# One more pair by seven products, and engine programs written run by run, in a two-group matrix kernel

## The chip, the cores and the metric

One NeuronCore of a Trainium2 chip runs the kernel. The metric is the device time of one execution in microseconds, the median of several runs.

## The reference

The input r_x holds 1024 rows of 10240 numbers; each row is two vectors of 5120. Both go through the same two layers, are joined and go through a third, and a dot product ends it:

```python
x = x.reshape(-1, 2 * F)                      # F = 5120
x1, x2 = (x[:, :F], x[:, F:])
h1 = leaky_relu(layer_norm(x1 @ W1.T))        # W1: 256 x 5120, leaky_relu(x) = max(0.05 x, x)
h2 = leaky_relu(layer_norm(x2 @ W1.T))
h1 = leaky_relu(layer_norm(h1 @ W2.T))        # W2: 64 x 256
h2 = leaky_relu(layer_norm(h2 @ W2.T))
h = jnp.concatenate([h1, h2], axis=-1)
h = leaky_relu(layer_norm(h @ W3.T))          # W3: 8 x 128
return h @ W4.T                               # W4: 1 x 8
```

Layer norm subtracts the mean over the outputs and divides by the root of the mean square. Nearly all of the arithmetic is the first layer, 2048 vectors of 5120 times W1.

## The kernel before

**Tiling.** F is cut into 20 pairs of two blocks of 128. The 2048 vectors are two groups (g) of 1024, each of two blocks (b) of NC = 512 columns; the 256 outputs are two halves (m) of 128. For a group and a pair, TensorE multiplies a 2 x 2 matrix of weight blocks with a 2 x 2 matrix of x blocks and sums over the 20 pairs in PSUM, whose eight banks hold 128 x 512 each.

**Precision.** Each operand is split into a rounded high part and a low part, and each product is three matmuls: high by high, high by low, low by high. ScalarE makes the high part by a cast (`hi`, L443), VectorE the low part by a subtraction (`lo`, L524). Weights are centred first: ScalarE takes the mean (L399) and subtracts it (L405), VectorE makes the low part (L539).

**Two kinds of pair.** An E unit multiplies plainly: eight products, 24 matmuls, in two halves (c) of 12. An S unit uses seven products of sums (Strassen-Winograd), 21 matmuls: first R, three raw blocks, nine matmuls; then T, four sums of blocks, twelve matmuls. VectorE makes the sums of x (L575, L580, L585) and of the weights (L551, L556, L561); their high parts are `hi` (1478 ns for R, 1903 for T) and L427 for the weight, their low parts `lo` and L530. The products of S pairs go to banks P1, P5, P6, P7 and others and are put together at a group's end by four additions (`seven_into`, L593 to L601), to which the eight-product banks are added (`eight_into`, L607).

**Order.** `ORDER` lists the units; TensorE takes them as they stand: group 0 is E E, four times S E E, S E, S E E L; group 1 is F, E, eight times S E, D. L is the last E of group 0 (its two halves are cast into T's buffer), F the first of group 1, after which layer 2 of group 0 runs, and D is two pairs at the end. Group 0 prepares weights; group 1 finds them in SBUF, save those of the `MIXED` pairs that are S only there. All engines follow one count of parts: `hi_ready`, `lo_ready` and `used` are one semaphore each, so ScalarE, VectorE and TensorE must take the parts in the same order. In one pass of ScalarE's loop stand: cast of unit u's first part, weight of the next unit, cast of u's second part, weight high part of the next. In VectorE's pass before an S: low part of the first half, the sums of the S with the second half's low part before the last of them, then the S's weight low part.

**Buffers.** The parts have one pair of high and low buffers each: R, T, E0, E1. `hi` waits (`used`) until TensorE is done with the old content. Raw x lies in rings of two (S, 1 MB) and four (halves of E, 512 KB), raw weights in a ring of three (256 KB). SP's queue issues all loads but the first half of x, which ScalarE's issues; each waits for the low part of the ring's earlier owner.

**What the prediction's steps touch:** `ORDER` and `plan`; the programs of ScalarE (`start_w`, `end_w`, `hi`, `copy_p1`) and VectorE (`lo`, `w_lo`, the sums, `seven_into`, `centre_w23`), and SP's loads. `centre_w23` centres the small weights, after unit 8.

Of the kernel before, what the change touches and what calls it, by code (L numbers as in the profile page):

```python
# [12 lines left out]
P = 128  # L13
# [12 lines left out]
SEVEN = 6  # L26
MIXED = 2
# [7 lines left out]
W23_UNIT = 8  # L35
# [7 lines left out]
ORDER = ("EE" + "SEE" * 4 + "SE" + "SEEL", "FE" + "SE" * 8 + "D")  # L43
# [26 lines left out]
class Part:  # L70

    n: int
# [9 lines left out]
def plan():  # L82
    units, latest, count, halves, sevens = [], {}, 0, 0, 0
    for g, order in enumerate(ORDER):
        seen = {"S": 0, "E": 0}
        for kind in order:
# [16 lines left out]
            parts = []  # L103
            for buffer, p, c, blocks in wanted:
                parts.append(Part(count, g, buffer, p, c, blocks, latest.get(buffer, 0), halves))
                count += 1
                if kind != "S" and blocks[-1] == 1:
                    halves += 1
            for part in parts:
                latest[part.buffer] = part.n + 1  # L110
# [16 lines left out]
def following(u):  # L127
    return UNITS[u.n + 1] if u.n + 1 < len(UNITS) else None
# [11 lines left out]
def rec_kernel(nc, x, w1, w2, w3, w4, out):  # L140
    with ExitStack() as ctx:
# [88 lines left out]
        hi_ready = sem("hi_ready")  # L230
        lo_ready = sem("lo_ready")
        used = sem("used")
# [32 lines left out]
        def w_slot(u):  # L265
            return W_AT[u.n] % W_RING, 16 * (W_AT[u.n] // W_RING + 1)

# [31 lines left out]
        def _(sp):  # L299
# [13 lines left out]
            def load_seven(nth):  # L313
                if nth >= len(SEVENS):
                    return
                u = SEVENS[nth]
                s, landed = s_slot(u)
                if nth >= S_RING:
                    sp.wait_ge(lo_ready, SEVENS[nth - S_RING].parts[0].n + 1)
                sp.dma_start(xs_raw[:, s, :], x[u.g, u.pair]).then_inc(xs_landed[s], 16)  # L320

            def load_half(half):
                if half not in HALVES:
                    return
                part = HALVES[half]
                s, landed = e_slot(half)
                block0 = 2 * part.c
                if half >= E_RING:
                    sp.wait_ge(lo_ready, HALVES[half - E_RING].n + 1)
                sp.dma_start(xe_raw[:, s, :], x[part.g, part.pair, :, block0 * NC:(block0 + 2) * NC])\  # L330
                    .then_inc(xe_landed[s], 16)
# [6 lines left out]
            load_half(2)  # L338
            load_half(3)
            load_w(2)  # L340
            load_seven(0)
            for u in UNITS:
                if u.kind == "S":
                    load_seven(u.nth + S_RING)
                else:
                    load_half(u.parts[-2].half + E_RING)
                if u.n == 0:
                    load_w(W_RING)
                    load_seven(1)
                if u.n + 1 + W_RING < len(FIRST):  # L350
                    load_w(u.n + 1 + W_RING)
                if u.kind != "S":
                    load_half(u.parts[-1].half + E_RING)
                if u.n == 4:
# [4 lines left out]
                if u.n == len(FIRST) + 6:  # L359
# [36 lines left out]
        def _(act):  # L396
# [11 lines left out]
            def start_w(u):  # L408
                s, landed = w_slot(u)
# [14 lines left out]
            def end_w(u):  # L424
                if u.kind == "S":
# [3 lines left out]
            def hi(u, part):  # L429
                if u.kind != "S":  # L430
                    s, landed = e_slot(part.half)
                    if part.n == 0:
# [8 lines left out]
                if part.before:  # L441
                    act.wait_ge(used, part.before)
                act.copy(hi_of(u, part), raw_of(u, part)).then_inc(hi_ready, 1)  # L443

            def copy_p1(g):
                act.wait_ge(used, last_seven(g).parts[0].n + 1)
# [4 lines left out]
            def leak1(g, b, m):  # L451
                act.wait_ge(drained, 5 * g + 2 + 2 * b + m)
                act.activation(a1[:, b, m, :], h1[:, b, m, :], ACT.Prelu, alpha=LEAK).then_inc(a1_ready, 1)  # L453

# [11 lines left out]
            act.dma_start(xe_raw[:, 0, 0:NC], x[0, u.pair, :, 0:NC]).then_inc(first_x_landed, 16)  # L466
            act.dma_start(xe_raw[:, 0, NC:], x[0, u.pair, :, NC:2 * NC]).then_inc(xe_landed[0], 16)
# [10 lines left out]
            for u in UNITS[1:]:  # L478
                nxt = following(u)
                prepare_w = nxt and nxt.n in W_AT  # L480
                hi(u, u.parts[0])
                if u.n == len(FIRST) - 2:
                    copy_p1(0)
                if prepare_w:
                    start_w(nxt)
                hi(u, u.parts[1])
                if prepare_w:
                    end_w(nxt)
                if u.kind == "F":
                    for b in range(B):  # L490
                        for m in range(M):
                            leak1(u.g - 1, b, m)
                        for m in range(M):
                            square1(u.g - 1, b, m)
                if u.n == len(FIRST) + 1:
                    for b in range(B):
                        layer2_end(0, b)
                if u.kind == "D":
                    copy_p1(u.g)
                    hi(u, u.parts[2])  # L500
                    hi(u, u.parts[3])
# [12 lines left out]
        def _(dve):  # L514
# [7 lines left out]
            def lo(u, part):  # L522
                dve.wait_ge(hi_ready, part.n + 1)
                dve.tensor_tensor(lo_of(u, part), raw_of(u, part), hi_of(u, part).bitcast(F32), ALU.subtract)\  # L524
                    .then_inc(lo_ready, 1)

            def w_lo(u):
                if u.kind == "S":
# [37 lines left out]
            def two_sums(u):  # L566
                s, landed = s_slot(u)
                dve.wait_ge(xs_landed[s], landed)
                if u.nth:
                    dve.wait_ge(lo_ready, SEVENS[u.nth - 1].parts[1].n + 1)  # L570
# [16 lines left out]

            def seven_into(g, k):

                if k == 0:  # L590
                    dve.wait_ge(used, last_seven(g).parts[1].n + 1)
# [5 lines left out]
                if k == 2:  # L597
                    dve.tensor_tensor(h1[:, 0, 1, :], h1[:, 1, 1, :], acc[:, P7, :], ALU.add).then_inc(h1_step, 1)
# [70 lines left out]
            for u in UNITS[1:]:  # L669
                nxt = following(u)  # L670
                prepare_w = nxt and nxt.n in W_AT
                g = u.g
                if u.kind == "S":
                    lo(u, u.parts[0])
                    if prepare_w:
                        w_lo(nxt)
                    lo(u, u.parts[1])
                elif u.kind == "D":
                    for part in u.parts:
                        lo(u, part)  # L680
                    for k in range(4):
                        seven_into(g, k)
                elif u.n == len(FIRST) - 2:
                    lo(u, u.parts[0])
                    w_lo(nxt)
                    seven_into(g, 0)
                    seven_into(g, 1)
                    lo(u, u.parts[1])
                    seven_into(g, 2)
                    seven_into(g, 3)  # L690
                elif u.n == len(FIRST) + 1:
                    lo(u, u.parts[0])
                    lo(u, u.parts[1])
                    two_sums(nxt)
                    third_sum(nxt)
                    fourth_sum(nxt)
                elif nxt.kind == "S":
                    lo(u, u.parts[0])
                    if prepare_w:
                        w_two_sums(nxt)  # L700
                    two_sums(nxt)
# [280 lines left out]
```

## Time and profile before

| what | value |
|---|---|
| median of 3 runs | 254.1 us (253.92 to 254.76) |
| the profiled execution | 255.57 us |
| its span, first to last instruction | 253.8 us |
| PE busy | 233.0 us, 1022 matmuls |
| DVE (VectorE) busy | 195.6 us |
| ACT (ScalarE) busy | 153.5 us |
| mean granted clock of TensorE | 0.984 |

PE's busy time counts matmuls to their modelled ends, which overlap, so 233.0 is not a measure of how full it is; the distance from start to start is. A number in brackets in a timeline is the idle time before the instruction and who ended it.

### The profile page before, as it was taken

How to read it: one execution, taken by the hardware profiler on the slowest of the kernel's cores; microseconds unless marked ns; L12 is line 12 of the kernel's file. 1: busy time of each engine (PE TensorE's matmuls, PEld its weight loads, DVE VectorE, ACT ScalarE, POOL GpSimd, SP SyncE). 2: the span in 40 equal slices, each digit the busy share in tenths (PEclk: the TensorE clock that was granted, in tenths of full speed). 3: DMA queues.
4: the chain of work that ended last, by engine and by line, in shares of the span. 5: the costliest groups of instructions: out<-in, count | busy, mean ns of one | idle time of the engine just before them, and what ended most of it. 6: DMA issues, size and time to landing. Idle time of an engine off the chain costs nothing.

```text
span 253.8 us, 2896 instructions
## 1 busy us (share of the span) xinstructions
PE 233.0 (92%) x1022; PEld 183.5 (72%) x1022; DVE 195.6 (77%) x250; ACT 153.5 (60%) x239; POOL 8.3 (3%) x16
## 2 busy tenths in 40 slices
PE   5987997997997988989999999999999999999982
PEld 1765875875865866868677888888888888888662
DVE  1689599598699499985965878999887999619434
ACT  4869379379478577858476536464546677333620
POOL 1000000000000000000000031000000000000023
PEclk9999999999999999999999999999999999999985
DMA  5999747656666567665482543787666425220000
GB/s 182 414 407 393 256 145 275 217 176 240 205 206 216 209 203 233 192 224 171 159 262 87 181 149 111 256 316 269 209 211 223 154 79 165 80 85 4 0 0 1
DMA packets 13550, 47.99 MB, mean 189 GB/s; under 512 B 1888, under 2 KB 2272, under 8 KB 11744
## 3 DMA queue, kind: packets, MB, share of 16 engines
q1 hardware_dynamic: 13248, 47.29, 54.4%
q10 hardware_dynamic: 288, 0.52, 0.7%
q8 instruction: 8, 0.13, 0.2%
q14 instruction: 6, 0.05, 0.1%
HBM read 47.80 MB, written 0.00 MB: 188 GB/s over the span
## 4 chain that ended last, share of the span: by engine, by line
PE 52%; DVE 18%; ACT 18%; issue 5%; DMA 4%; SPq 1%; POOL 1%; POOLq 0%; ACTq 0%; DVEq 0%
PE acc L766 48%; DVE xt_lo L524 7%; ACT xt_hi L443 4%; DMA xs_raw<-x 4%; ACT xr_hi L443 3%; ACT unused L399 3%; DVE x_sum L575 3%; ACT xe_hi L443 2%; PE acc L897 2%; DVE xe_lo L524 2%; ACT we_hi L405 1%; DVE x_sum L580 1%; ACT stage L405 1%; PE acc L885 1%; ACT x_sum L453 1%
## 5 line engine op out<-in xcount | busy, mean ns | idle before, releaser
L443 ACT CAST xe_hi<-xe_raw 128x1024 fp32r<-128x1024 f32 (+1 forms) x49 | 50.5, 1031 | 47.8 <-PE acc L766 44.0
L524 DVE TENSOR_TENSOR xe_lo<-xe_raw,xe_hi 128x1024 fp32r<-128x1024 f32 (+1 forms) x49 | 58.8, 1199 | 26.0 <-ACT xe_hi L443 25.9
L766 PE MATMUL acc<-xe_lo,we_hi 128*128 128x512 f32 x176 | 69.0, 392 | 1.1 <-DVE xe_lo L524 1.1
L766 PE MATMUL acc<-xe_hi,we_lo 128*128 128x512 f32 x176 | 68.6, 390 | 0.0
L766 PE MATMUL acc<-xe_hi,we_hi 128*128 128x512 f32 x176 | 48.3, 391 | 0.3 <-PE acc L766 0.3
L766 PEld LDWEIGHTS acc<-xe_lo,we_hi 128*128 128x128 f32 x176 | 33.0, 188 | 9.8 <-issue 3.1
L766 PEld LDWEIGHTS acc<-xe_hi,we_hi 128*128 128x128 f32 x176 | 32.9, 188 | 7.4 <-issue 0.7
L766 PEld LDWEIGHTS acc<-xe_hi,we_lo 128*128 128x128 f32 x176 | 33.0, 188 | 6.8
L524 DVE TENSOR_TENSOR xt_lo<-x_sum,xt_hi 128x2048 fp32r<-128x2048 f32 x14 | 32.1, 2290 | 7.3 <-ACT xt_hi L443 7.3
L443 ACT CAST xt_hi<-x_sum 128x2048 fp32r<-128x2048 f32 x14 | 26.6, 1903 | 8.9 <-DVE x_sum L585 5.2
L766 PE MATMUL acc<-xt_lo,ws_hi 128*128 128x512 f32 x56 | 22.3, 398 | 6.7 <-DVE xt_lo L524 6.7
L443 ACT CAST xr_hi<-xs_raw 128x1536 fp32r<-128x1536 f32 x14 | 20.7, 1478 | 6.8 <-PE acc L766 6.8
L524 DVE TENSOR_TENSOR xr_lo<-xs_raw,xr_hi 128x1536 fp32r<-128x1536 f32 x14 | 24.5, 1752 | 0.0
L766 PE MATMUL acc<-xt_hi,ws_lo 128*128 128x512 f32 x56 | 21.9, 390 | 0.0
L766 PE MATMUL acc<-xr_lo,ws_hi 128*128 128x512 f32 x42 | 16.9, 402 | 2.5 <-DVE xr_lo L524 2.5
L766 PEld LDWEIGHTS acc<-xt_lo,ws_hi 128*128 128x128 f32 x56 | 10.5, 188 | 11.1 <-issue 9.1
L399 ACT ACTIVATE unused<-stage 128x256 f32<-128x256 f32 x40 | 16.3, 408 | 1.7 <-DMA stage<-w 1.6
L575 DVE TENSOR_TENSOR x_sum<-xs_raw 128x1024 f32<-128x1024 f32 x14 | 17.1, 1219 | 0.3 <-DMA xs_raw<-x 0.3
L766 PE MATMUL acc<-xr_hi,ws_lo 128*128 128x512 f32 x42 | 16.4, 392 | 0.0
L427 ACT CAST ws_hi<-stage 128x896 fp32r<-128x896 f32 x8 | 7.6, 945 | 13.4 <-DVE stage L561 13.4
L766 PE MATMUL acc<-xt_hi,ws_hi 128*128 128x512 f32 x56 | 15.1, 391 | 0.0
L379 POOL TENSOR_TENSOR inv<-var,minus_half 128x4 f32<-128x4 f32 (+1 forms) x3 | 4.9, 1625 | 239.4 <-DVE var L622 239.4
(87 smaller groups left out, 269.3 us busy)
## 6 DMA issues: line engine op xcount, KB each, us to landing
xe_raw<-x SPq DMA_DIRECT2D x51, 512.0 KB, 3.9
xs_raw<-x SPq DMA_DIRECT2D x14, 1024.0 KB, 5.1
stage<-w SPq DMA_DIRECT2D x21, 256.0 KB, 4.7
xe_raw<-x ACTq DMA_DIRECT2D x2, 256.0 KB, 5.0
stage<-w SPq DMA_DIRECT2D x2, 128.0 KB, 4.2
w_raw<-w SPq DMA_DIRECT2D x1, 64.0 KB, 3.3
w_sb<-w SPq DMA_DIRECT2D x1, 8.0 KB, 3.1
w_sb<-w SPq DMA_DIRECT2D x1, 16.0 KB, 3.0
```

The source lines that it names most:

```text
L379: pool.tensor_tensor(inv12[:, a * J:b * J], var12[:, a * J:b * J], minus_half[:, a * J:b * J], ALU.pow)\
L399: act.activation(unused[:, c, :], w_raw[:, s, c * N1:(c + 1) * N1], ACT.Copy, scale=-1.0 / N1, accum_out=w_mean[:, u.pair, c:c + 1]).then_ ...
L405: return act.activation(to, w_raw[:, s, c * N1:(c + 1) * N1], ACT.Identity, bias=w_mean[:, u.pair, c:c + 1], scale=1.0)
L427: act.copy(ws_hi[:, u.pair, :], w_mid[:, P:]).then_inc(w_hi_ready, 1)
L443: act.copy(hi_of(u, part), raw_of(u, part)).then_inc(hi_ready, 1)
L453: act.activation(a1[:, b, m, :], h1[:, b, m, :], ACT.Prelu, alpha=LEAK).then_inc(a1_ready, 1)
L524: dve.tensor_tensor(lo_of(u, part), raw_of(u, part), hi_of(u, part).bitcast(F32), ALU.subtract)\
L575: dve.tensor_tensor(x_sum[:, 0:2 * NC].rearrange("p (a n) -> p a n", a=2), raw[:, :, 0, :], b12, ALU.add).then_inc(two_sums_ready, 1)
L580: dve.tensor_tensor(x_sum[:, 2 * NC:3 * NC], x_sum[:, 0:NC], x_block(u, 2), ALU.add)\
L766: return pe.matmul(acc[:, bank, :], w, x, start=first, stop=True, skip_group_check=True)
L885: ins = pe.matmul(h2_ps[b][h * N2:(h + 1) * N2, :], w2_sb[:, m, :], a1[:, b, m, h * T * P:(h + 1) * T * P], start=(m == 0), stop=(m == M - ...
L897: ins = pe.matmul(acc[:, var1_bank[g][b], k:k + 1], sq1_sum[b][:, j * P:(j + 1) * P], ones[:], start=True, stop=True)
```

## The change

Group 0 has seven instead of six S pairs, and group 1 one instead of two mixed ones (`SEVEN`, `MIXED`); group 1 has eight as before. Group 0's order becomes E E, twice S E E, four times S E, S E E L. The one count of parts becomes one per buffer (`hi_ready[buffer]` and so on), so an engine's program may leave TensorE's order. The programs are written by runs: a run is the E units up to an S, that S, and the units after it. ScalarE casts R of the S, then, in turn, the halves of the run's second E, the S's weight and T, and then the weights and halves of the next run's first E and the weight of the next S. VectorE makes all sums of the S first, then the low parts in that order. At the groups' crossing `seven_into` stands ahead of the low parts, at the end too, and ScalarE's leaks stand ahead of its squares. Layer 3 of group 0 stands between two halves of an E. The first half of x is loaded by SP's queue, and the halves of an E lie one after another in DRAM. `centre_w23` moves to the run of the fifth S.

```diff
-SEVEN = 6
-MIXED = 2
+SEVEN = 7
+MIXED = 1
-ORDER = ("EE" + "SEE" * 4 + "SE" + "SEEL", "FE" + "SE" * 8 + "D")
+ORDER = ("EE" + "SEE" * 2 + "SE" * 4 + "SEEL", "FE" + "SE" * 8 + "D")
...
+def runs():
+
+    starts = [0] + [u.n + 1 for u in SEVENS]
+    ends = [u.n for u in SEVENS] + [len(UNITS)]
+    es = [UNITS[a:b] for a, b in zip(starts, ends)]
+    return list(zip(es, SEVENS + [None], es[1:] + [[]]))
...
+def crosses(run):
+
+    return run[0].g != run[-1].g
...
-        hi_ready = sem("hi_ready")
-        lo_ready = sem("lo_ready")
-        used = sem("used")
+        hi_ready = {buffer: sem("hi_ready_" + buffer) for buffer in x_hi}
+        lo_ready = {buffer: sem("lo_ready_" + buffer) for buffer in x_hi}
+        used = {buffer: sem("used_" + buffer) for buffer in x_hi}
...
+            first_half = x_half_of(0, pair, 0)
             sp.dma_start(w_raw[:, 0, 0:N1], w1[pair, :, 0:N1]).then_inc(first_w_landed, 16)
+            sp.dma_start(xe_raw[:, 0, 0:NC], first_half[:, 0:NC]).then_inc(first_x_landed, 16)
             sp.dma_start(w_raw[:, 0, N1:], w1[pair, :, N1:]).then_inc(w_landed[0], 16)
+            sp.dma_start(xe_raw[:, 0, NC:], first_half[:, NC:]).then_inc(xe_landed[0], 16)
...
+            for i, (es, n, after) in enumerate(RUNS):
+                if not n:
+                    copy_p1(GROUPS - 1)
+                    for part in es[1].parts:
+                        hi(es[1], part)
+                    break
+                if crosses(es):
+                    copy_p1(es[0].g)
+                    start_w(es[2])
+                    for k in range(2):
+                        for u in es[1:3]:
+                            hi(u, u.parts[k])
+                    for part in es[3].parts:
+                        hi(es[3], part)
+                    layer1_end(es[0].g)
+                    for part in es[4].parts:
+                        hi(es[4], part)
...
+                    hi(n, n.parts[0])
+                    hi(n, n.parts[1])
+                else:
+                    if i:
+                        hi(n, n.parts[0])
+                    for j, u in enumerate(es[1:], 1):
+                        if j > 1:
+                            start_w(u)
+                        hi(u, u.parts[0])
+                        if i == 0:
+                            start_w(n)
+                        elif j == 1:
+                            end_w(n)
+                            hi(n, n.parts[1])
+                        hi(u, u.parts[1])
+                    if i == 0:
+                        hi(n, n.parts[0])
+                    if i == 0 or len(es) == 1:
+                        end_w(n)
+                        hi(n, n.parts[1])
+                start_w(after[0])
+                hi(after[0], after[0].parts[0])
+                if len(after) > 1:
+                    start_w(after[1])
+                hi(after[0], after[0].parts[1])
+                start_w(RUNS[i + 1][1])
...
+            for i, (es, n, after) in enumerate(RUNS):
+                g = es[0].g
+                if not n:
                     for k in range(4):
                         seven_into(g, k)
...
+                    for part in es[1].parts:
+                        lo(es[1], part)
+                    break
+                if crosses(es):
                     seven_into(g, 0)
                     seven_into(g, 1)
...
+                    w_lo(es[2])
                     seven_into(g, 2)
                     seven_into(g, 3)
...
+                    for k in range(2):
+                        for u in es[1:3]:
+                            lo(u, u.parts[k])
+                    for part in es[3].parts:
+                        lo(es[3], part)
...
+                elif i == 0:
+                    lo(es[1], es[1].parts[0])
+                    lo(es[1], es[1].parts[1])
+                    sums(n)
+                    lo(n, n.parts[0])
+                else:
+                    sums(n)
+                    for j, u in enumerate(es[1:], 1):
+                        if j > 1:
+                            w_lo(u)
+                        lo(u, u.parts[0])
+                        if j == 1:
+                            lo(n, n.parts[0])
+                        lo(u, u.parts[1])
+                    if len(es) == 1:
+                        lo(n, n.parts[0])
+                w_lo(n)
+                lo(n, n.parts[1])
...
+                w_lo(after[0])
+                lo(after[0], after[0].parts[0])
+                if crosses(es):
                     layer3(1, 0, B, small[:, B * J:B * J + B * J * N3])
+                lo(after[0], after[0].parts[1])
...
+                if len(after) > 1:
+                    w_lo(after[1])
+                if es[0].n == W23_UNIT + 2:
+                    centre_w23()
...
+    for g, sevens in enumerate((SEVEN, BOTH)):
+
+        x[g, sevens:] = x[g, sevens:].reshape(-1, P, 2, 2 * NC).transpose(0, 2, 1, 3).reshape(-1, P, 4, NC)
+    x = x.reshape(GROUPS, PAIRS, P * 4 * NC)
```

`sums` is the six additions of an S, weights and x in turn; `layer1_end` is the four leaks and then the four squares.

## Rows read from the trace of the kernel before

**Rows 1.** The chain that ended last, merged: start, length, what
```profile
147.21 79.05 PE acc L766 x348
```

**Rows 2.** Table of stages: stretch, its length, busy time (instructions) by engine, clock, DMA, GB/s
```profile
38.52:56.90 18.38, 16.48 (x70) 12.69 (x69) 14.34 (x18) 12.92 (x26) 0.00 (x0) 1.00 0.66 219
...
93.66:106.03 12.37, 10.77 (x47) 8.26 (x45) 11.79 (x14) 9.90 (x20) 0.00 (x0) 1.00 0.70 220
```

**Rows 3.** Waits of the whole span: engine and tile, awaited; total us, times, longest
```profile
ACT xe_hi L443 <- PE acc L766: 44.0, 22, 6.4
DVE xe_lo L524 <- ACT xe_hi L443: 25.9, 12, 6.3
```

**Rows 4.** Timeline of PE: start, length, line, operation [idle before]
```profile
108.17 1.09 PE L766 MATMUL acc<-xt_hi,ws_hi 128*128 128x512 f32 x4
110.38 0.47 PE L766 MATMUL acc<-xt_lo,ws_hi 128*128 128x512 f32 x1 [1.13 <-DVE xt_lo L524]
```

**Rows 5.** Timeline of VectorE in the SE cycle, same columns
```profile
99.58 0.42 DVE L551 TENSOR_TENSOR stage<-stage 128x256 f32<-128x256 f32 x1
...
103.79 1.08 DVE L530 TENSOR_TENSOR ws_lo<-stage,ws_hi 128x896 fp32r<-128x896 f32 x1
104.79 1.75 DVE L524 TENSOR_TENSOR xr_lo<-xs_raw,xr_hi 128x1536 fp32r<-128x1536 f32 x1
106.46 0.88 DVE L539 SCALAR_TENSOR_TENSOR we_lo<-stage,w_mean,we_hi 128x256 fp32r<-128x256 f32 x2
107.94 2.29 DVE L524 TENSOR_TENSOR xt_lo<-x_sum,xt_hi 128x2048 fp32r<-128x2048 f32 x1 [0.60 <-ACT xt_hi L443]
110.15 1.22 DVE L524 TENSOR_TENSOR xe_lo<-xe_raw,xe_hi 128x1024 fp32r<-128x1024 f32 x1
111.29 0.87 DVE L539 SCALAR_TENSOR_TENSOR we_lo<-stage,w_mean,we_hi 128x256 fp32r<-128x256 f32 x2
112.08 1.22 DVE L524 TENSOR_TENSOR xe_lo<-xe_raw,xe_hi 128x1024 fp32r<-128x1024 f32 x1
```

**Rows 6.** Timeline of ScalarE in the SE cycle
```profile
102.17 0.95 ACT L427 CAST ws_hi<-stage 128x896 fp32r<-128x896 f32 x1 [2.47 <-DVE stage L561]
103.02 1.48 ACT L443 CAST xr_hi<-xs_raw 128x1536 fp32r<-128x1536 f32 x1
104.40 0.42 ACT L399 ACTIVATE unused<-stage 128x256 f32<-128x256 f32 x1
...
106.01 1.90 ACT L443 CAST xt_hi<-x_sum 128x2048 fp32r<-128x2048 f32 x1
107.81 1.06 ACT L443 CAST xe_hi<-xe_raw 128x1024 fp32r<-128x1024 f32 x1
108.75 0.43 ACT L399 ACTIVATE unused<-stage 128x256 f32<-128x256 f32 x1
```

**Rows 7.** The page's list of DMA issues: count, KB each, median us to landing
```profile
stage<-w SPq DMA_DIRECT2D x21, 256.0 KB, 4.7
```

**Rows 8.** Timelines of ScalarE and VectorE at the start
```profile
13.85 1.04 ACT L443 CAST xe_hi<-xe_raw 128x1024 fp32r<-128x1024 f32 x1
...
16.87 1.22 DVE L524 TENSOR_TENSOR xe_lo<-xe_raw,xe_hi 128x1024 fp32r<-128x1024 f32 x1
```

**Rows 9.** Timeline of VectorE: first step of the small weights' centring, first after it
```profile
61.70 0.28 DVE L649 TENSOR_REDUCE w_mean<-w_raw 128x2 f32<-128x128 f32 x1
...
62.97 1.22 DVE L524 TENSOR_TENSOR xe_lo<-xe_raw,xe_hi 128x1024 fp32r<-128x1024 f32 x1
```

**Rows 10.** Timeline of PE: first products of unit F
```profile
130.46 0.70 PE L766 MATMUL acc<-xe_hi,we_hi 128*128 128x512 f32 x2 [0.30 <-PE acc L766]
```

**Rows 11.** Timeline of GpSimd after the crossing
```profile
148.15 2.48 POOL L379 TENSOR_TENSOR inv<-var,minus_half 128x8 f32<-128x8 f32 x1 [146.49 <-DVE var L622]
```

**Rows 12.** Timelines of VectorE and PE at the end
```profile
234.83 1.29 DVE L607 TENSOR_TENSOR stage<-acc,stage 128x512 f32<-128x512 f32 x2
...
233.79 0.39 PE L766 MATMUL acc<-xe_lo,we_hi 128*128 128x512 f32 x1
```

More of the change, by code:

```diff
@@ L82, in plan @@
 def plan():
-    units, latest, count, halves, sevens = [], {}, 0, 0, 0
+    units, made, halves, sevens = [], {}, 0, 0
     for g, order in enumerate(ORDER):
@@ L103, in plan @@
             parts = []
+            before = dict(made)
             for buffer, p, c, blocks in wanted:
-                parts.append(Part(count, g, buffer, p, c, blocks, latest.get(buffer, 0), halves))
-                count += 1
+                made[buffer] = made.get(buffer, 0) + 1
+                parts.append(Part(made[buffer], g, buffer, p, c, blocks, before.get(buffer, 0), halves))
                 if kind != "S" and blocks[-1] == 1:
                     halves += 1
-            for part in parts:
-                latest[part.buffer] = part.n + 1
             units.append(Unit(len(units), g, kind, pair, sevens, parts))
@@ L124 @@
 W_SEVENS = {u.n: i for i, u in enumerate(v for v in W_WORK if v.kind == "S")}
[L127 to L128 removed]
+def runs():
[3 more added lines that the diff above has]
+    return list(zip(es, SEVENS + [None], es[1:] + [[]]))
+RUNS = runs()
+def crosses(run):
+    return run[0].g != run[-1].g
 def last_seven(g):
@@ L338, in _ @@
             load_half(2)
+            load_w(2)
             load_half(3)
-            load_w(2)
             load_seven(0)
[L342 to L354, printed above, removed]
+            load_w_after(UNITS[0])
+            load_halves(UNITS[0], 1)
+            load_halves(UNITS[0], 2)
+            load_seven(1)
+            load_w_after(UNITS[1])
+            for es, n, after in RUNS:
+                if n:
+                    load_w_after(n)
+                for j, u in enumerate(es[1:], 1):
+                    if j > 1:
+                        load_w_after(u)
+                    for k in range(len(u.parts)):
+                        load_halves(u, k)
+                        if n and j == 1 and k == 0 and not crosses(es):
+                            load_seven(n.nth + S_RING)
+                if n and (len(es) == 1 or crosses(es)):
+                    load_seven(n.nth + S_RING)
+                for j, u in enumerate(after[:2]):
+                    load_w_after(u)
+                    if j == 0:
+                        for k in range(len(u.parts)):
+                            load_halves(u, k)
+                if es[0].n == W23_UNIT:
                     sp.dma_start(w2_raw[:], w2).then_inc(small_landed, 16)
@@ L431, in hi @@
                     s, landed = e_slot(part.half)
-                    if part.n == 0:
+                    if part is UNITS[0].parts[0]:
                         act.wait_ge(first_x_landed, 16)
@@ L441, in hi @@
                 if part.before:
-                    act.wait_ge(used, part.before)
-                act.copy(hi_of(u, part), raw_of(u, part)).then_inc(hi_ready, 1)
+                    act.wait_ge(used[part.buffer], part.before)
+                act.copy(hi_of(u, part), raw_of(u, part)).then_inc(hi_ready[part.buffer], 1)
             def copy_p1(g):
-                act.wait_ge(used, last_seven(g).parts[0].n + 1)
+                act.wait_ge(used["R"], last_seven(g).parts[0].nth)
                 if g == 0:
@@ L586, in fourth_sum, with sums @@
                     .then_inc(sums_ready, 1)
+            def sums(u):
+                new_w = u.n in W_AT
+                if new_w:
+                    w_two_sums(u)
+                two_sums(u)
+                if new_w:
+                    w_third_sum(u)
+                third_sum(u)
+                if new_w:
+                    w_fourth_sum(u)
+                fourth_sum(u)
             def seven_into(g, k):
                 if k == 0:
-                    dve.wait_ge(used, last_seven(g).parts[1].n + 1)
+                    dve.wait_ge(used["T"], last_seven(g).parts[1].nth)
                     dve.wait_ge(p1_copied, g + 1)
@@ L803, in seven @@
                         ins = multiply(u.g, bank, w_of(ws_lo, n), x_of(x_hi, k))
-                    ins.then_inc(used, 1)
+                    ins.then_inc(used[part.buffer], 1)
             def w_of(buffers, part, m):
@@ L832, in eight @@
                             ins = e_lo(u, part, b, m)
-                    ins.then_inc(used, 1)
+                    ins.then_inc(used[part.buffer], 1)
             def first_eight(u):
@@ L844, in first_eight @@
                             ins = e_lo(u, part, b, m)
-                    ins.then_inc(used, 1)
+                    ins.then_inc(used[part.buffer], 1)
             def last_eight(u):
```

135 lines of the change are left out of this document (45 added, 90 removed).

## The prediction

> **What bounds the kernel now.** I read the table of stages first. In the second half of the program TensorE runs without a gap: 348 matmuls of 128x512 in 79.05 us, 0.227 us each [rows 1]. So a half pair of eight-product work (12 matmuls) is 2.72 us, an eight-product pair (E) 5.45, a seven-product pair (S) with 21 matmuls 4.77, and a cycle SEE should take 69 x 0.227 = 15.7 us. A cycle of the first group takes 18.38 us for that [rows 2], and there are four such cycles, one SE cycle of 12.37 us (10.2 by count) and an end. The waits say why: ScalarE stands 44.0 us waiting for TensorE before it casts a half (xe_hi), and VectorE 25.9 us for that cast [rows 3]. A buffer of the high part is free only once TensorE has used it; ScalarE's program has the half next, so the seven-product pair's weight and its cast stand behind it, and VectorE, which has the sums after the half, idles too and then does everything late. TensorE shows the end of it: the four high products of a pair's sums start at 108.17, but the low ones only at 110.38 instead of 109.08 [rows 4]. With such gaps at R, T and the second half, the cycle loses 2.7 us. None of the three engines is full: the lost time is order.
>
> **What VectorE and ScalarE need at least.** Starts are closer than durations (a 1.22 us subtraction is followed after 1.14), so I take start to start. VectorE [rows 5]: all sums of an S with its weight 103.79 - 99.58 = 4.21, less one half's subtraction of 1.14 that lies among them, 3.07; weight low part 1.00; R low 1.67; T low 2.21: together 7.95 for an S. An E is 0.79 for the weight and 2 x 1.14 for the halves, 3.07. ScalarE [rows 6]: weight high part 0.85, R 1.38, mean and centre 1.61, T 1.80, a half 0.94; 5.64 for an S, 3.49 for an E. Per SEE: TensorE 15.7, VectorE 14.1, ScalarE 12.6. Per SE: 10.2, 11.0, 9.1. So with a good order SEE is TensorE's, SE is VectorE's.
>
> **The change, part by part.** (1) One E of group 0 becomes an S: TensorE 3 matmuls less, -0.7 us; VectorE 7.95 - 3.07 = 4.9 more; ScalarE 2.1 more. In group 1 the reverse happens only to weights: one seven-product weight less, where VectorE has time. (2) The order of units becomes two SEE cycles and four SE cycles. (3) In the new programs the sums of an S stand before the half of the E ahead of it, and the casts of the first E after an S stand before that run ends. VectorE has then 3.07 us of work in the place where it idles now. (4) A count per buffer costs no instruction; it lets the orders differ from TensorE's. (5) The halves lie together in DRAM: 4 KB per partition as before. I take nothing; a load of a weight lands in 4.7 us [rows 7], and in the walk below every load is asked for over 8 us ahead, which hides a change either way. (6) The first x loads go from ScalarE's queue to SP's, two issues ahead of the others (about 0.4 us each). The first cast stands behind the weight's centring and waits for that; the S's first 1 MB comes after 3.75 MB of loads in either order. I take 0; the bounds are -0.3 and +0.9 us, the two issues, for both engines stand at the start.
>
> **The walk through group 0.** Today the low part of the last half before the first S stands behind that S's first sums: cast at 13.85 to 14.89, subtraction only at 16.87 [rows 8]. After the change it goes at 14.93, and VectorE starts the sums at 16.07. From there to the end of the last S's T low part VectorE has seven S, 7 x 7.95 = 55.7; eight E between them, 24.6; and the centring of the small weights, moved into this stretch, 1.27 [rows 9]: 16.07 + 81.5 = 97.6 if it never waits. I walked the three programs step by step with the steps above, 0.04 us from ScalarE to VectorE (T cast ends 107.91, subtraction starts 107.94 [rows 5, 6]), 0.15 from VectorE to TensorE (110.23 to 110.38 [rows 4, 5]), and, an estimate, a buffer free 0.25 after the start of TensorE's next product. VectorE waits 0.6 and 0.4 us in the first SEE cycle (casts behind ScalarE's weights), and 0.8 and 0.8 in the second (buffers not yet free), 2.6 in all. So T low ends at 100.2, where it ends for the sixth S today at 110.2. The seven S end on TensorE at 26.1, 42.9, 58.5, 68.8, 79.0, 91.4 and 102.4: cycles of 16.7 and 15.7, two of 10.2 in which VectorE's lead of 1.9 us is used up (0.8 each), one of 12.4 (0.8, the centring and the rest of the lead), one of 11.0. ScalarE's own loop in SE, from a ready weight over the sums (2.6), weight high, T, two weights and two halves is 10.5 us, under VectorE's 11.0, so it does not set the cycle.
> Then E, E, L. VectorE now puts the four additions of group 0's seven-product banks and L's weight ahead of the second E's low parts; with ScalarE's copy of bank P1 waiting on the last weight, the first low part comes at 109.7 where TensorE wants it at 108.8: 1.0 us lost. Behind that copy on ScalarE are L's weight and four casts; TensorE waits for these, and the 1.0 contains it. L starts at 114.4 and F at 119.8; F starts at 130.46 now [rows 10]. That is -10.6 us.
>
> **Crossing and group 1.** The additions to the eight-product banks, squares and layer 2 keep their order against TensorE. After S7 the layer 3 steps now stand between the two halves of an E, behind GpSimd's 2.48 us power [rows 11]: the second half's low part ends about 1.3 us before it is wanted, the next S's T low part about 0.3 after: +0.3 (bounds 0 and 2.5, if all of the power falls on the path). The rest of group 1 is VectorE 9 to 10.2 us against 10.2: no gap, as now.
>
> **The end.** The four additions move ahead of the last low parts. Today the first addition to an eight-product bank starts at 234.83 behind them, though the product that it needs starts at 233.79 and ends near 234.2 [rows 12]. It can go at 234.25: -0.5 us, next limited by that product.
>
> The sum: -10.6 + 0.3 - 0.5 = -10.8. The profiled execution took 255.57 us with a span of 253.8; the median is 254.1. So the span becomes 243.0, the profiled execution about 244.8, the median 243.3.
>
> **A rule weighed against a row.** In rows 5 an instruction starts 0.08 us before its predecessor's duration is over, also where sums wait for sums with other work between. The Trainium skill, "VectorE: DVE Perf Modes", section "The DRAIN you can't avoid", says that the next operation does not start until the pipeline has emptied, and adds that one that is not held starts earlier. The steps of this trace bear out the second half. If the first held for the new order, rival A would come.
>
> **Rivals.** (A) VectorE pays full durations, or waits as much again between steps, since almost each of its steps now has another engine's result in front of it. By durations an S is 8.7 us and an E 3.3: 7 x 0.75 + 8 x 0.25 = 7.2 us more, of which the 2.6 of waiting take about 1.7: +5.5, 248.8 us. For it: VectorE is the bound and nothing hides it. Against: in the SE stretch of the trace the steps stay close.
> (B) The change does not do what it says, and ends slower: the gap at each S stays. ScalarE still waits for TensorE's buffers, and its weight and T cast stand behind that wait, so the low T part stays last. Then there are seven gaps of 2.7 instead of six: +2.7 - 0.7 = +2.0, 256.1 us. It decides from 2.4 us per S ((6 x 2.7 + 0.7) / 7); at exactly that the time is unchanged. For it: 44.0 us of such waits today. Against: VectorE has the sums to do meanwhile, and the walk finds T ready ahead in three of the seven.
> (C) Loads late. A weight is asked for when the slot three units back is done: in the walk at 28.5 for 37.2, 8.7 us ahead. Landing takes 4.7 us [rows 7]. Each landing over 8.7 us stretches some six rounds of the ring; at 10.5 us the whole gain is gone, at 11 it is 257 us. Against: the rate rises only from 219 GB/s [rows 2] to about 240 (3.75 MB in 15.7 us).
>
> **How the numbers follow.** The walk holds: 0.71, own range 240.7 (VectorE never waits) to 246.4 (start +0.9, crossing +2.2). A: 0.14. B: 0.08, half of it with gaps that leave the time as it is. C: 0.03. Over half the gain lost by something else, 249 to 253: 0.04. The range, 240.7 to 249.0, takes in the walk and A. This kernel can tell about 0.3% (0.8 us) from no change. Faster by over 0.3%: 0.71 + 0.14 + 0.04 = 0.89; within 0.3%: 0.04, of B; slower: 0.04 of B and 0.03 of C, 0.07.
>
> **What would show it.** PE's stretch from one S to the next: 15.7 us in SEE, 11 in SE; VectorE over 95% busy from 55 to 100 us; no idle of VectorE of 3 us before a half. F's first product near 120 us. Group 1 without gaps, but for 0.3 us after S7. If VectorE's steps in SE sum to 12 us, A. If its idle before halves is still over 2 us per cycle, B. If ScalarE waits for w or x, C.

## The result, and the profile after

The changed kernel takes 244.96 us (244.87 to 245.41, 4 runs) against 254.43 (253.92 to 255.15, 4 runs): a ratio of 0.9629, 95% interval 0.9600 to 0.9658, 9.5 us less. Forecast were 243.3 us and a range of 240.7 to 249.0. The profiled execution took 244.94 us, with a span of 243.1 where 243.0 had been walked out.

The table of stages of the profile after, columns as in [rows 2] (stretch, its length, busy time with instructions for PE, PE's weight load, VectorE, ScalarE, GpSimd, clock, DMA, GB/s):

```profile
37.90:53.63 15.73, 15.73 (x70) 12.87 (x69) 14.24 (x18) 11.92 (x22) 0.00 (x0) 1.00 0.76 251
53.63:63.84 10.21, 10.21 (x46) 8.45 (x45) 10.21 (x14) 7.54 (x15) 0.00 (x0) 1.00 0.69 234
...
55.00:100.00 45.00, 43.04 (x187) 34.44 (x186) 44.93 (x60) 35.96 (x68) 0.00 (x0) 1.00 0.70 233
```

The first line is a whole SEE cycle: 15.73 us where [rows 2] has 18.38. The last holds the four SE cycles: VectorE is busy 44.93 of 45.00 us. It has become the bound there, and TensorE is what idles (43.04 busy). The waits of the whole span (engine and tile, awaited; total, times, longest) answer [rows 3]:

```profile
ACT xe_hi L479 <- PE acc L845: 22.6, 14, 4.9
ACT xt_hi L479 <- DVE x_sum L650: 17.4, 7, 5.1
DVE xe_lo L587 <- ACT xe_hi L479: 15.4, 19, 1.7
PEld acc L845 <- DVE ws_lo L595: 4.6, 4, 1.8
PE acc L845 <- DVE ws_lo L595: 3.2, 3, 1.3
```

ScalarE's wait for TensorE is halved, VectorE's wait for that cast falls from 25.9 to 15.4 us and has no longer stretch than 1.7. New are the last two lines: TensorE waits for the low part of an S's weight. They show a wait that my walk did not have (below).

VectorE's timeline of one SE cycle (start, length, line, operation [idle before]), from the first weight sum to the next one, as in [rows 5]:

```profile
57.74 0.42 DVE L616 TENSOR_TENSOR stage<-stage 128x256 f32<-128x256 f32 x1
...
60.82 1.75 DVE L587 TENSOR_TENSOR xr_lo<-xs_raw,xr_hi 128x1536 fp32r<-128x1536 f32 x1
62.49 1.08 DVE L595 TENSOR_TENSOR ws_lo<-stage,ws_hi 128x896 fp32r<-128x896 f32 x1
63.49 2.28 DVE L587 TENSOR_TENSOR xt_lo<-x_sum,xt_hi 128x2048 fp32r<-128x2048 f32 x1
65.70 0.87 DVE L604 SCALAR_TENSOR_TENSOR we_lo<-stage,w_mean,we_hi 128x256 fp32r<-128x256 f32 x2
66.49 2.35 DVE L587 TENSOR_TENSOR xe_lo<-xe_raw,xe_hi 128x1024 fp32r<-128x1024 f32 x2
68.76 0.41 DVE L616 TENSOR_TENSOR stage<-stage 128x256 f32<-128x256 f32 x1
```

The cycle is 68.76 - 57.74 = 11.02 us without a gap, and the sums take 3.08. Only TensorE's waits are left to show; its timeline at the first, the sixth and the seventh S and at the crossing:

```profile
21.14 0.64 PE L845 MATMUL acc<-xr_lo,ws_hi 128*128 128x512 f32 x1 [1.33 <-DVE ws_lo L595]
...
86.92 0.50 PE L845 MATMUL acc<-xr_lo,ws_hi 128*128 128x512 f32 x1 [1.33 <-DVE ws_lo L595]
...
97.94 0.50 PE L845 MATMUL acc<-xr_lo,ws_hi 128*128 128x512 f32 x1 [0.50 <-DVE ws_lo L595]
...
110.24 0.47 PE L845 MATMUL acc<-xe_lo,we_hi 128*128 128x512 f32 x1 [1.17 <-DVE xe_lo L587]
...
120.79 0.70 PE L845 MATMUL acc<-xe_hi,we_hi 128*128 128x512 f32 x2 [0.30 <-PE acc L845]
```

The last line is F's first product, at 130.46 in [rows 10]. From the first product of group 1's first S (the prediction's S7: it counts the S from zero there) the chain that ended last holds one piece without a gap; for [rows 1]:

```profile
137.53 90.06 PE acc L845 x396
```

396 products in 90.06 us are 0.227 each, as before.

### The profile page after: what moved, and what is told of

It reads as the page before. It is cut to its first block, busy times and chain, and to the rows that moved or that the text cites. A ratio compares the mean times of both kernels' runs of the same rounds, so it can differ in the third digit from the quotient of the medians.

```text
span 243.1 us, 2884 instructions
## 1 busy us (share of the span) xinstructions
PE 229.5 (94%) x1019; PEld 182.6 (75%) x1019; DVE 198.8 (82%) x251; ACT 153.0 (63%) x237; POOL 8.3 (3%) x16
## 4 chain that ended last, share of the span: by engine, by line
PE 61%; DVE 25%; ACT 7%; issue 3%; DMA 2%; POOL 1%; SPq 1%; POOLq 0%; DVEq 0%; ACTq 0%
PE acc L845 57%; DVE xe_lo L587 5%; DVE xt_lo L587 4%; DVE xr_lo L587 3%; ACT xe_hi L479 2%; DVE x_sum L640 2%; DMA xe_raw<-x 2%; DVE ws_lo L595 2%; DVE we_lo L604 2%; PE acc L976 2%; ACT unused L433 1%; DVE x_sum L645 1%; PE acc L964 1%; ACT xt_hi L479 1%; DVE x_sum L650 1%
## 5 line engine op out<-in xcount | busy, mean ns | idle before, releaser
L587 DVE TENSOR_TENSOR xe_lo<-xe_raw,xe_hi 128x1024 fp32r<-128x1024 f32 (+1 forms) x47 | 55.6, 1198 | 15.4 <-ACT xe_hi L479 15.4
L479 ACT CAST xe_hi<-xe_raw 128x1024 fp32r<-128x1024 f32 (+1 forms) x47 | 47.8, 1026 | 28.8 <-PE acc L845 22.6
L479 ACT CAST xt_hi<-x_sum 128x2048 fp32r<-128x2048 f32 x15 | 28.6, 1910 | 17.4 <-DVE x_sum L650 17.4
L587 DVE TENSOR_TENSOR xt_lo<-x_sum,xt_hi 128x2048 fp32r<-128x2048 f32 x15 | 34.3, 2287 | 2.2 <-ACT xt_hi L479 2.2
L587 DVE TENSOR_TENSOR xr_lo<-xs_raw,xr_hi 128x1536 fp32r<-128x1536 f32 x15 | 26.2, 1750 | 0.0
L845 PE MATMUL acc<-xr_lo,ws_hi 128*128 128x512 f32 x45 | 18.5, 411 | 3.2 <-DVE ws_lo L595 3.2
L845 PE MATMUL acc<-xr_hi,ws_lo 128*128 128x512 f32 x45 | 18.3, 406 | 0.0
L845 PE MATMUL acc<-xt_hi,ws_hi 128*128 128x512 f32 x60 | 16.6, 399 | 0.0
L845 PE MATMUL acc<-xr_hi,ws_hi 128*128 128x512 f32 x45 | 13.0, 397 | 1.1 <-ACT ws_hi L463 0.9
L845 PEld LDWEIGHTS acc<-xt_hi,ws_hi 128*128 128x128 f32 x60 | 11.8, 196 | 2.6
```

The source lines that it names most:

```text
L479: act.copy(hi_of(u, part), raw_of(u, part)).then_inc(hi_ready[part.buffer], 1)
L845: return pe.matmul(acc[:, bank, :], w, x, start=first, stop=True, skip_group_check=True)
```

## The experiments

In all of them ratios are against the kernel before on the same chip. Single executions of one kernel spread over 1 to 2.7 us here, so times decide only where the intervals stand apart, and else I compare stretches inside profiles. Much of the spread is in two places that no experiment here aims at: the start, and the clock in the last 8 us (last section).

**1. The new programs with six S.** The kernel takes all of the change but the seventh pair.

```diff
-SEVEN = 7
-MIXED = 1
+SEVEN = 6
+MIXED = 2
-ORDER = ("EE" + "SEE" * 2 + "SE" * 4 + "SEEL", ...
+ORDER = ("EE" + "SEE" * 4 + "SE" + "SEEL", ...
-                if es[0].n == W23_UNIT + 2:
+                if es[0].n == W23_UNIT + 3:
```

> The new programs with six S pairs and the old order of units. Theory (VectorE bounds group 0, so the seventh S costs 2.2 us: TensorE would need 4 x 15.7 + 10.2 = 73.0 us from the end of the first S to the end of the last, where the changed kernel took 102.2 - 26.9 = 75.2): 242.8 us, that is faster than the changed kernel. Rival (the seventh S saves its three matmuls): 245.7 us.

Measured: 242.34 us, 0.9511 (0.9474 to 0.9548), clearly under the changed kernel's 0.9629 (0.9600 to 0.9658): 2.6 us by the medians, 3.0 by the ratios. By the profiles the seventh S itself costs less. From the first S's T low part to the last S's it is 75.22 us with six and 76.79 with seven, and from there to layer 2 of group 0 both take the same, so 1.6 us are the seventh S's. The rest of the 2.9 us between the two spans is a start 0.7 earlier and 0.6 in the last 8 us, where the clock fell sooner in the changed kernel's profile. Table of stages from 55 to 97 us, where here SEE cycles run, and one SE cycle from 83 to 95:

```profile
55.00:97.00 42.00, 41.79 (x184) 34.00 (x183) 38.98 (x53) 31.29 (x59) 0.00 (x0) 1.00 0.73 236
```

VectorE is busy 38.98 of 42 and TensorE has hardly a gap.

**2. The old programs with seven S** in the new order of units.

```diff
-SEVEN = 6
-MIXED = 2
+SEVEN = 7
+MIXED = 1
-ORDER = ("EE" + "SEE" * 4 + "SE" + "SEEL", ...
+ORDER = ("EE" + "SEE" * 2 + "SE" * 4 + "SEEL", ...
```

> The old programs with seven S pairs and the new order of units. Theory (the gain is the programs'; under the old ones a cycle SEE takes 18.4 us and an SE 11.7): last S ends 2 x 18.4 + 4 x 11.7 = 83.6 us after the first instead of 4 x 18.4 + 11.7 = 85.3: 252.7 us. Rival (the gap stays at every S, 2.7 us each): 256 us. If the order of units and the seventh S brought most of the gain: under 249.

Measured: 253.97 us, 0.9969 (0.9949 to 0.9990), 0.8 us faster. VectorE's T low parts:

```profile
59.41 2.29 DVE L524 TENSOR_TENSOR xt_lo<-x_sum,xt_hi 128x2048 fp32r<-128x2048 f32 x1 [0.58 <-ACT xt_hi L443]
...
72.36 2.29 DVE L524 TENSOR_TENSOR xt_lo<-x_sum,xt_hi 128x2048 fp32r<-128x2048 f32 x1 [0.59 <-ACT xt_hi L443]
...
84.06 2.29 DVE L524 TENSOR_TENSOR xt_lo<-x_sum,xt_hi 128x2048 fp32r<-128x2048 f32 x1 [0.60 <-ACT xt_hi L443]
```

The second SE cycle is the 11.7 us expected, the first 12.95: the centring of the small weights stands in it, and I had not counted that. It is the 1.3 us by which the kernel is slower than the 252.7 expected. So the gain of the change is the programs', and under them the seventh pair takes some of it back, while under the old ones it gave a little.

**3. Spare work for VectorE** in the SE runs of group 0, and in a second kernel in those of group 1 (`== 1` in place of `== 0`).

```diff
+                if es[0].g == 0 and len(es) == 1:
+                    dve.tensor_tensor(spare[:], ws_hi[:, 0, 0:NC].bitcast(F32), ws_hi[:, 0, 0:NC].bitcast(F32), ALU.add)
```

> The changed kernel with one addition of 128x512 on VectorE, of no use, at the end of each run with one E in group 0 (four of them, 0.61 us each from start to start). Theory (VectorE bounds that stretch): +2.4 us less what little lead is left, 246.9 to 247.4. Rival (ScalarE's loop or the weight loads bound it): 245.0 to 245.5.

> The same addition in the runs with one E of group 1 instead. TensorE bounds that stretch and VectorE has 9.1 to 10.2 us of work in 10.2: no change, 245.0, or up to 0.6 more where the last S also brings a weight.

Measured: 246.29 us, 0.9669 (0.9628 to 0.9710), and 244.83, 0.9611 (0.9570 to 0.9652). The first interval overlaps the changed kernel's, so I read the profile. T's low parts of the third and of the seventh S end 45.31 us apart in the changed kernel and 47.12 apart here; with the addition in group 1, 45.32. Only three of the four additions lie between the two (I had counted four): 1.81 us, 0.60 each, all of it on the path.

```profile
65.95 2.35 DVE L588 TENSOR_TENSOR xe_lo<-xe_raw,xe_hi 128x1024 fp32r<-128x1024 f32 x2
68.22 0.68 DVE L814 TENSOR_TENSOR spare<-ws_hi 128x512 f32<-128x512 f32 x1
68.82 0.41 DVE L617 TENSOR_TENSOR stage<-stage 128x256 f32<-128x256 f32 x1
```

**4. The centring moved** from the SE stretch to the crossing.

```diff
-                    for part in es[3].parts:
-                        lo(es[3], part)
+                    lo(es[3], es[3].parts[0])
+                    centre_w23()
+                    lo(es[3], es[3].parts[1])
...
-                if es[0].n == W23_UNIT + 2:
-                    centre_w23()
```

> The changed kernel with the centring of the small weights (1.27 us on VectorE) moved out of the SE stretch to the crossing, between the two halves of F, where VectorE waits 1.56 us. Theory (VectorE bounds the SE stretch): 243.7 us. Rival: no change, 245.0.

Measured: 242.93 us, 0.9523 (0.9494 to 0.9551). The stretch from the third to the seventh S is 44.07 instead of 45.31 us, 1.24 less, as expected for 1.27. The spans of the two profiled executions differ by 1.4 us: these 1.24, 0.55 more in the last 8 us, where the clock fell sooner in the changed kernel's, less 0.4 for a later start. The time fell by more, 2.0 us by the medians and 2.7 by the ratios; what is above 1.4 of it lies in executions without a profile and stays open.

**5. The first loads of x.** In the kernel before, they are moved to SP's queue; in the changed kernel, back to ScalarE's.

```diff
-            sp.dma_start(xe_raw[:, 0, 0:NC], first_half[:, 0:NC]).then_inc(first_x_landed, 16)
-            sp.dma_start(xe_raw[:, 0, NC:], first_half[:, NC:]).then_inc(xe_landed[0], 16)
...
+            act.dma_start(xe_raw[:, 0, 0:NC], first_half[:, 0:NC]).then_inc(first_x_landed, 16)
+            act.dma_start(xe_raw[:, 0, NC:], first_half[:, NC:]).then_inc(xe_landed[0], 16)
             act.wait_ge(first_w_landed, 16)
```

> The kernel before with only the two first loads of x moved to SP's queue. First product 1.4 us earlier as in the changed kernel. If that carries through: 253.0 us. If the first S's 1 MB load and VectorE's order behind it set the stage: 254.2, no change.

> The changed kernel with the two first loads of x issued by ScalarE again. If the earlier start (0.8 us on VectorE at the first sums) carries through the stretch that VectorE bounds: +0.6 to +0.8 us, 245.7. If it is lost in waits: 245.0.

Measured: 254.47 us, 0.9993 (0.9970 to 1.0016), no change, and 244.65, 0.9591 (0.9536 to 0.9645), which is not apart from 0.9629. In the first, TensorE starts at 5.34 instead of 6.26, and the first T low part ends at 25.23 instead of 25.03: the start was hidden. In the second, VectorE's first sums start at 14.79, 0.8 earlier than the 15.59 of the changed kernel, the opposite of what I expected. But over the other profiles with the loads on SP's queue that start lies anywhere from 14.86 to 16.80, and in experiment 9 it is 16.30 with the loads on ScalarE's. With the loads on SP's queue, what sets it is the landing of the load of the second half of x, waited for by ScalarE's third cast: in all nine profiles of the new programs the sums follow that cast by 7.7 to 7.8 us, and the landing differs from run to run. With the loads on ScalarE's queue it is something else: here that cast waits for nothing, and in experiment 9 the cast after it waits 0.99 us for TensorE. Which queue is better stays open.

**6. Products of zeros while TensorE waits at the first S.**

```diff
+                    if u.nth == 0 and part.buffer == "R":
+                        for _ in range(7):
+                            pe.matmul(acc[:, P5, :], zeros[:, 0:P], zeros[:], start=True, stop=True)
                     lo_ready_for(u, part)
```

> The changed kernel with seven products of zeros (bf16) into a bank not yet in use, while TensorE waits at the first S for R's low part. Theory: the clock stays at 2.4 GHz from 21 to 25 us, TensorE is 1.6 us earlier at the end of the first S, and nearly all of it is lost by the fifth S, where VectorE is late anyway: 244.4 to 245.0. Rival (the low clock is on the path): 243.4.

The stretch from 21 to 25 us in the changed kernel and here (the clock is the third number from the end):

```profile
21.00:25.00 4.00, 3.86 (x10) 3.05 (x11) 4.00 (x5) 4.00 (x13) 0.00 (x0) 0.57 0.97 353
```

```profile
21.00:25.00 4.00, 4.00 (x20) 2.64 (x18) 4.00 (x5) 4.00 (x12) 0.00 (x0) 1.00 0.82 280
```

Measured: 244.68 us, 0.9594 (0.9546 to 0.9642), not apart in time. The clock stays up. TensorE ends the first S 2.05 us after VectorE's T low part, instead of 3.64: the 1.6 us expected. The T low parts of the first and third S are 30.81 us apart instead of 31.48, and the four cycles after them keep their length: 0.67 of the 1.6 us reach VectorE and stay. Variants whose program is the same up to there kept the clock without help (30.82 and 30.83 in the profiles of experiment 3), so it is not shown that the products of zeros did it.

**7. The wait that I had missed.** `lo_ready_for` asks for the weight's low part also before R's low products. Here VectorE makes it first.

```diff
                         if j == 1:
+                            w_lo(n)
                             lo(n, n.parts[0])
...
                     if len(es) == 1:
+                        w_lo(n)
                         lo(n, n.parts[0])
-                w_lo(n)
                 lo(n, n.parts[1])
```

> The changed kernel with an S's weight low part on VectorE ahead of R's low part. TensorE's low products of R need both, and the profile puts 3.2 us of its waits on the weight's. Theory (T's low part comes last anyway and VectorE bounds the cycle; the weight's high part is ready only 0.5 us after the sums): an SE cycle of 11.5 instead of 11.0 us, 246 to 247 us. Rival (the wait for the weight's low part is on the path): 243 to 244.

Measured: 246.48 us, 0.9688 (0.9656 to 0.9720), slower than the changed kernel by 1.5 us; the two intervals just touch, so the cycle decides.

```profile
60.00 0.68 DVE L650 TENSOR_TENSOR x_sum<-x_sum,xs_raw 128x512 f32<-128x512 f32 x1
61.09 1.09 DVE L595 TENSOR_TENSOR ws_lo<-stage,ws_hi 128x896 fp32r<-128x896 f32 x1 [0.41 <-ACT ws_hi L463]
62.09 1.75 DVE L587 TENSOR_TENSOR xr_lo<-xs_raw,xr_hi 128x1536 fp32r<-128x1536 f32 x1
```

VectorE idles 0.41 us and the cycle becomes 11.51 us. The 3.2 us that the profile books on the weight's low part were not to be had there: TensorE is late because VectorE is.

**8. The crossing.** The second E's halves first, the last two additions behind all low parts that L needs.

```diff
                     copy_p1(es[0].g)
+                    hi(es[1], es[1].parts[0])
                     start_w(es[2])
...
                     seven_into(g, 1)
+                    lo(es[1], es[1].parts[0])
                     w_lo(es[2])
+                    lo(es[1], es[1].parts[1])
+                    for part in es[2].parts:
+                        lo(es[2], part)
                     seven_into(g, 2)
                     seven_into(g, 3)
...
```

> The changed kernel; at the crossing ScalarE casts the second E's first half ahead of L's weight, and VectorE makes that half's low part after the first two additions, L's weight low part and the other low parts next, and the last two additions behind them. Theory (the one wait of TensorE there, 1.17 us for that low part, is the order's): it goes, 243.8 us. Rival (it is the copy of bank P1 that waits for the last weight, so it stays): 245.0.

Measured: 242.44 us, 0.9529 (0.9507 to 0.9550). All of TensorE's waits from 98 to 125 us:

```profile
98.11 0.50 PE L847 MATMUL acc<-xr_lo,ws_hi 128*128 128x512 f32 x1 [0.46 <-DVE ws_lo L596]
119.15 0.70 PE L847 MATMUL acc<-xe_hi,we_hi 128*128 128x512 f32 x2 [0.30 <-PE acc L847]
```

The wait of 1.17 us is gone, and so is that of 0.15 ahead of it. From the end of the last S's T low part to layer 2 it is 24.55 us instead of 26.36, 1.8 less. The spans of the two profiled executions differ by 2.2 us: these 1.8, 0.6 because this one kept the clock at the first S, 0.6 in the last 8 us, less 0.8 for a later start.

**9. The three together:** six S, the centring late, the crossing in its new order; and the same with the first x loads on ScalarE's queue.

> The new programs with six S, the centring between F's halves, and the new order at the crossing. Theory: from 242.3 (six S) less 1.1 for the crossing and up to 0.5 for the centring, where VectorE has some lead in SEE cycles: 240.9 us. Rival (the gains overlap): 241.8 or more.

> The same with the two first loads of x issued by ScalarE. Theory (the second half's load is issued 0.9 us later behind them on SP's queue, and the chain of casts on ScalarE to the first sums hangs on its landing): 0.5 to 0.9 us faster than the kernel with the loads on SP, 240.2. Rival (the first product's start counts, 0.9 us later): 241.5 or more.

Measured: 240.44 us, 0.9446 (0.9422 to 0.9470), and 239.34, 0.9428 (0.9393 to 0.9464). Both beat the kernel before and the changed one, and the first is apart from every single variant above; they are not apart from each other. TensorE's stretch in the first of them:

```profile
55.00:97.00 42.00, 42.00 (x186) 34.50 (x186) 39.07 (x47) 32.56 (x62) 0.00 (x0) 1.00 0.75 250
```

```profile
20.74 95.39 PE acc L846 x411
```

From the low products of the first S to F TensorE is the chain that ends last.

## Why the prediction was right, point by point

**The walk through group 0** held almost step by step. When the seven S end on TensorE:

| S | walked | measured |
|---|---|---|
| first | 26.1 | 26.9 |
| second | 42.9 | 42.7 |
| third | 58.5 | 58.4 |
| fourth | 68.8 | 68.6 |
| fifth | 79.0 | 78.9 |
| sixth | 91.4 | 91.2 |
| seventh | 102.4 | 102.2 |

VectorE ends the last T low part at 100.08, for 100.2. Steps taken from start to start carry over to a new order: 11.02 us per SE cycle for the 11.02 of the sum. Experiments 3 and 4 show that the stretch of the SE cycles is VectorE's, to 0.05 us. But that the end was met to 0.1 us is in part luck. VectorE began the first sums at 15.25, not at 16.07, and then took 84.8 us to the end of the last T low part, where the walk had 84.1. The start differs by up to 1.9 us from profile to profile; of the 0.7 us, nearly all is what the low clock at the first S cost (0.67 in experiment 6), which the walk did not have.

**Where steps failed inside it.** The missed wait (experiment 7) cost nothing in the SE cycles, since T's low part, which follows the weight's by 2.2 us, comes as late for TensorE. At the first S TensorE waited 1.33 us, until the weight's low part, which comes 1.0 us behind R's, and then its clock was low: it ended the first S 0.8 us later than walked, although VectorE had begun its sums 0.8 us earlier. On TensorE that was made good by the second S.

**The seventh pair.** I priced it at -0.7 us for TensorE and 4.9 more for VectorE, and the walk has both, but I never asked what six pairs would give under the new programs. Experiment 1 does: 1.6 us less by the profiles, 2.6 by the medians. The gain came in spite of the first half of the title's change.

**The crossing** was mis-sized by 0.95 us: F starts at 120.79, not 119.8. The low part of the second E's half came 0.5 later than walked (110.24 for 109.7), since VectorE waited 0.51 us for a cast and 0.78 for the copy of P1. And F waits 0.3 us, 0.46 from start to start, for L's own last product, today too; I had compared a start with that wait to one without. After S7 the 0.3 us for GpSimd's power did not show: no wait of TensorE is left there. From S7 on the change is -9.7 us, not -10.3.

**The end** gave -0.4 for -0.5. The first addition to an eight-product bank starts at 224.53, 10.3 earlier than in [rows 12], 0.6 more than at S7; but the products behind the last of layer 1 start only 10.05 earlier (232.30 for 242.35), since TensorE's own products are next in line.

**From span to median.** The span fell by 10.7, the walk said 10.8, and yet the median fell only by 9.5. Two errors make up for each other in the span, and that is luck. The walk had 0.7 us too much of a gain, 0.6 of it on the crossing and S7. About as much came back from the clock: the last sum of variances (eight products of 128x1) took 1.86 us in the profile of before and 1.25 after, because the clock fell to 1.2 GHz earlier in the former (granted 0.50 from 245.5 on there, 1.00 up to 236.0 here). Its line in the kernel before, in the changed one and in the old programs with seven S:

```profile
245.72 1.86 PE L897 MATMUL acc<-ones,stage 128*128 128x1 f32 x8 [1.01 <-DVE stage L612]
...
235.67 1.25 PE L976 MATMUL acc<-ones,stage 128*128 128x1 f32 x8 [1.01 <-DVE stage L692]
...
245.28 1.05 PE L897 MATMUL acc<-ones,stage 128*128 128x1 f32 x8 [1.01 <-DVE stage L612]
```

That is no effect of the change: nine of the other twelve profiles show 1.05, of old and of new programs, and one of a new program (experiment 6) 1.86. So -9.7 at S7, -0.4 at the end and -0.6 of the clock are the 10.7.

From these products to the end of the span it is 8.1 us in the profile of before, 7.4 after, and 6.8 in that of the old programs with seven S, whose execution stands at its median. The profiled execution of before stood 1.5 us above the median of 254.1 that the prediction had (1.1 above the 254.43 measured later), and that of after at its own. I took the difference of spans off the median as if both profiled executions were typical. The forecast of the profiled execution, 244.8, came to 0.1 us (244.94); the 1.7 us between 243.3 and 244.96 are that step's, and the 1.3 us by which the last stretch of before's profile is longer than 6.8 are most of it.

**The rivals.** A (full durations) is refuted by the cycle of 11.02. B (the gap stays) is refuted for the new programs, and experiment 2 shows the gap of the old ones at seven S: even there the kernel did not become slower. C (late loads) did not come: ScalarE waits 6.2 us for x in all, five times, of which the start has 1.7 and the crossing the rest, where F's halves were ready before TensorE wanted them, and for a weight once, 0.8 us at the start. The rate in a SEE cycle rose to 251 GB/s, not to about 240: the walk's 3.75 MB are binary. Of the section "The DRAIN you can't avoid" of the Trainium skill's page "VectorE: DVE Perf Modes", the first half (the next operation waits until the pipeline is empty) would make this cycle 12.1 us, an estimate from the full durations of its thirteen instructions; the trace, with 11.02, agrees with the second half (one that is not held starts earlier).

**What was not taken apart.** Experiments 1 and 2 show that the gain is the new programs'. They do not say how much of it each part has: the sums ahead of the half, the count per buffer, the casts moved ahead, the halves' new place in DRAM. Only for the last does a number speak: ScalarE waited 3.4 us for halves of x in the profile of before and 6.2 after, so a shorter wait for loads is not where the gain is. That the sums' place closes the gap rests on the waits, and on the walk, which came out cycle by cycle.

## What to carry to other kernels

When three engines hand work round a ring of single buffers and none is full, the gap is in the order of each program: put work that depends on nothing recent where an engine would wait, and count readiness per buffer so that the orders may differ. Once the gaps are closed, add up each engine's steps per cycle anew before trading work between engines: a trade that saved TensorE 0.7 us cost VectorE 4.9, and at the new balance it lost about 2 us of a gain of 12. And before a difference of two profiles is moved to a median, see how each profiled execution stands to its own.

## What the runs showed of the hardware

TensorE's granted clock fell from 1.00 to 0.50 in the changed kernel's profile between 21.2 and 21.4 us, behind two idle stretches of 0.94 and 1.33 us with three products between them, for some 3 us (0.427 us a product instead of 0.227), with 0.67 us lost in the end. Other kernels with the same program up to there kept it at 1.00 behind idle stretches of the same length (0.96 and 1.34 us in experiment 3), and it stayed up in the one profile with seven products of zeros in the second stretch.

The load of the second half of x, the fifth of SP's queue, landed between 7.1 and 9.1 us over the nine profiles of new programs that issue it there (2.56 to 2.58 us), and the first sums moved with it, from 14.86 to 16.80. Over all profiles this is the largest difference that no edit aims at, 1.9 us; the last stretch with its clock has 1.3 (6.8 to 8.1), and the clock at the first S 0.7.
